# One operand of a product and a row maximum: the lattice filter of a language-model tower, rearranged between VectorE and GpSimd

## What is computed

```python
scores = q @ k.T / sqrt(64)                       # 1024 x 1024
int_scores = (abs(scores) * 1618.0).astype(int32)
penalty = where(int_scores % 3 == 0, 1 / PHI, 1)  # mod 9 in {0, 3, 6}
attn = softmax(scores * penalty)
attn = attn * (sin(C1 * attn) * exp(-attn * attn / PHI) + cos(C2 * attn))
ctx = attn @ v
```

## Time and profile before

| | us |
|---|---|
| median of 3 runs | 5857.68 |
| lowest, highest | 5852.5, 5871.76 |
| the profiled execution | 5868.64 |
| its span | 5866.9 |

### The profile page before, as it was taken

The page is one execution under the profiler, slowest core; times in us unless marked ns, Lnnn a source line. Parts: engine busy times, 40 slices in busy tenths (PEclk is TensorE's granted clock), DMA queues, the critical chain, the costliest instruction groups (busy, mean ns, idle before and its releaser), DMA issues. The chain is left out here.

```text
span 5866.9 us, 98280 instructions
## 1 busy us (share of the span) xinstructions
PE 4792.8 (82%) x27646; PEld 2698.8 (46%) x27689; DVE 4141.1 (71%) x7553; ACT 3988.8 (68%) x5466; POOL 3773.1 (64%) x3599
## 2 busy tenths in 40 slices
PE   2688888888888888888888888888888869997899
PEld 1344444444444444444444444444444436554566
DVE  2577777777777777777777777777777656665664
ACT  1577777777777777777777777777777734444332
POOL 4577777777777777777777777777777634443233
PEclk9799999999999999999999999999999879999999
DMA  0000000000000000000000000000000000000000
GB/s 5 23 9 8 8 8 8 8 9 8 10 8 8 8 8 8 8 8 8 9 8 10 8 8 8 8 8 8 8 9 8 4 9 1 2 2 15 3 6 7
DMA packets 34184, 45.24 MB, mean 8 GB/s; under 512 B 24521, under 2 KB 24585, under 8 KB 34058
## 3 DMA queue, kind: packets, MB, share of 16 engines
q1 hardware_dynamic: 32010, 43.49, 2.8%
q0 software_dynamic: 2048, 0.14, 0.1%
HBM read 39.40 MB, written 4.19 MB: 7 GB/s over the span
## 5 line engine op out<-in xcount | busy, mean ns | idle before, releaser
L588 PE MATMUL banks<-ident,att 128*128 128x128 f32 x8192 | 1148.2, 287 | 410.0 <-DVE ag L520 252.1
L588 PEld LDWEIGHTS banks<-ident,att 128*128 128x128 f32 x8192 | 944.6, 147 | 1004.1 <-DVE ag L520 616.9
L630 PE MATMUL banks<-kT,qT 128*128 128x512 f32 x2048 | 1144.8, 658 | 278.9 <-DVE mx L549 269.6
L390 POOL TENSOR_TENSOR sinb<-sinb,ag 128x1024 f32<-128x1024 f32 x512 | 1281.5, 2506 | 85.4 <-ACT sinb L461 70.4
L540 DVE SCALAR_TENSOR_TENSOR mag<-near,mag 128x512 f32<-128x512 int32 x1024 | 857.7, 842 | 483.6 <-POOL near L406 474.2
L400 POOL TENSOR_SCALAR mag<-mag 128x512 f32<-128x512 f32 x1024 | 689.5, 678 | 573.1 <-DVE mag L540 539.0
L647 PE MATMUL outp<-sinb,vo 128*64 128x512 f32 x2048 | 1046.3, 636 | 0.0
L647 PE MATMUL outp<-work,vo 128*64 128x512 f32 x2048 | 1046.3, 636 | 0.0
L406 POOL TENSOR_SCALAR near<-mag 128x512 int32<-128x512 f32 x1024 | 794.0, 775 | 363.9 <-ACT mag L479 300.3
L479 ACT ACTIVATE mag<-banks 128x512 f32<-128x512 f32 x1024 | 599.2, 592 | 283.1 <-PE banks L630 283.0
L497 DVE TENSOR_TENSOR work<-banks,work 128x1024 f32<-128x1024 f32 x512 | 625.1, 1221 | 192.8 <-ACT work L455 189.8
(11 more groups left out here) (198 smaller groups left out, 6357.7 us busy)
## 6 DMA issues: line engine op xcount, KB each, us to landing
x<-xT_dram SPq DMA_DIRECT2D x128, 256.0 KB, 3.5
xT_dram<-xT SPq DMA_DIRECT2D x8, 256.0 KB, 2.9
out<-hres SPq DMA_DIRECT2D x8, 256.0 KB, 2.6
base<-in_L_tok_turns,idx POOLq DMA_INDIRECT x64, 2.3
wqk<-in_L_attn_Wq SPq DMA_DIRECT2D x64, 16.0 KB
wqk<-in_L_attn_Wk SPq DMA_DIRECT2D x64, 16.0 KB
wqk<-in_L_attn_bq SPq DMA_DIRECT2D x64, 0.2 KB
wqk<-in_L_attn_bk SPq DMA_DIRECT2D x64, 0.2 KB
```

The costliest lines, as they stand in the source:

```text
L390: nc.gpsimd.tensor_tensor(sinb[:, k % RING], sinb[:, k % RING], ag[:, k], ALU.mult).then_inc(tmul, 1)
L588: mm = nc.tensor.matmul(turn_pair(k)[:, c, i * P:(i + 1) * P], att[:, p, 4 * half + i, kt * P:(kt + 1) * P], ident[:], is_transpose=True, ...
L630: nc.tensor.matmul(score_bank(n), qT[:, p, (n // 2) * P:(n // 2 + 1) * P], kT[:, p, (n % 2) * 512:(n % 2 + 1) * 512], start=True, stop=Tru ...
```

## The change

Three things on two engines:
- The PHI operation on POOL is gone. The comparison's 1.0 or 0.0 goes straight into a scalar_tensor_tensor on DVE, (mag + PHI) x score, which writes att and keeps no maximum.
- The maximum and the bias become one operation per block on 1024 columns of att: it multiplies by -EXPSCALE in place, and its reduction, a minimum, goes into nb. The exponential takes scale -1.0 for EXPSCALE. The tile mx is gone.
- All eight blocks are normalised on POOL; the two on DVE, their semaphore and their case are gone.

FILT moves from step +4 to +3, BIAS from +6 to +4.

```diff
-        ABS, RND, KEEP, FACT, FILT, BIAS = 1, 1, 2, 3, 4, 6
+        ABS, RND, KEEP, FILT, BIAS = 1, 1, 2, 3, 4
...
-                        if a - NORM in EXP and EXP.index(a - NORM) not in DVE_ROWS:
+                        if a - NORM in EXP:
                             j = EXP.index(a - NORM)
                             held(pool, recip, TB * g + j + 1)
                             nc.gpsimd.tensor_scalar(att[:, p, j], att[:, p, j], rs[:, j:j + 1], TURN,
                                                     ALU.mult, ALU.mult).then_inc(weights, 1)
-                        if a - FACT in SCORE:
-                            n = SCORE.index(a - FACT)
-                            held(pool, kept, NTILE * g + n + 1)
-                            nc.gpsimd.tensor_scalar(mag[:, n % 4], mag[:, n % 4], 1.0, PHI,
-                                                    ALU.mult, ALU.add).then_inc(factor, 1)
...
                             nc.scalar.activation(att[:, p, j], att[:, p, j], ACT.Exp,
-                                                 bias=nb[:, p, j:j + 1], scale=EXPSCALE,
+                                                 bias=nb[:, p, j:j + 1], scale=-1.0,
                                                  accum_out=ssum[:, j:j + 1]).then_inc(expd, 1)
...
-                        if a - NORM in EXP and EXP.index(a - NORM) in DVE_ROWS:
-                            j = EXP.index(a - NORM)
-                            wait(dve, recip, TB * g + j + 1)
-                            nc.vector.tensor_scalar(att[:, p, j], att[:, p, j], rs[:, j:j + 1], TURN,
-                                                    ALU.mult, ALU.mult).then_inc(weights2, 1)
...
-                            wait(dve, factor, NTILE * g + n + 1)
-                            wait(dve, filtered, NTILE * g + n)
+                            wait(dve, kept, NTILE * g + n + 1)
                             wait(dve, xpose, NX * (g - 1))
-                            dve.nop(nofuse=True)
-                            nc.vector.tensor_tensor_reduce(
-                                att[:, p, u, cols], mag[:, n % 4], score_bank(n), 1.0,
-                                mx[:, p, n - 1:n] if n % 2 else -3.0e38, ALU.mult, ALU.max,
-                                mx[:, p, n:n + 1]).then_inc(filtered, 1)
+                            nc.vector.scalar_tensor_tensor(att[:, p, u, cols], mag[:, n % 4], PHI, score_bank(n),
+                                                           ALU.add, ALU.mult).then_inc(filtered, 1)
...
                             wait(dve, filtered, NTILE * g + n + 1)
-                            nc.vector.tensor_scalar(nb[:, p, u:u + 1], mx[:, p, n:n + 1], -EXPSCALE, None,
-                                                    ALU.mult).then_inc(bias, 1)
+                            nc.vector.tensor_scalar(att[:, p, u], att[:, p, u], -EXPSCALE, 3.0e38, ALU.mult, ALU.min,
+                                                    accum_out=nb[:, p, u:u + 1]).then_inc(bias, 1)
...
-                wait(pe, weights, (TB - 2) * g + (TB // 2 - 1) * (half + 1))
-                wait(pe, weights2, 2 * g + half + 1)
+                wait(pe, weights, TB * g + TB // 2 * (half + 1))
```

More of the change, by code:

```diff
@@ L262, in lattice @@
         sinb = sb("sinb", [P, RING, S])
-        mx = sb("mx", [P, 2, 2 * TB])
         nb = sb("nb", [P, 2, TB])
@@ L294, in lattice @@
         NORM, TURNS = 1, 3
-        DVE_ROWS = (TB // 2 - 1, TB - 1)
         block = ctx.enter_context(nc.Block())
@@ L521, in iteration @@
                                                     ALU.mult).then_inc(agd, 1)
-                        if a - NORM in EXP and EXP.index(a - NORM) in DVE_ROWS:
-                            j = EXP.index(a - NORM)
-                            wait(dve, recip, TB * g + j + 1)
-                            nc.vector.tensor_scalar(att[:, p, j], att[:, p, j], rs[:, j:j + 1], TURN,
-                                                    ALU.mult, ALU.mult).then_inc(weights2, 1)
                         if a - TURNS in EXP:
                             j = EXP.index(a - TURNS)
-                            if j in DVE_ROWS:
-                                wait(dve, weights2, 2 * g + j // 4 + 1)
-                            else:
-                                wait(dve, weights, (TB - 2) * g + j + 1 - j // 4)
+                            wait(dve, weights, TB * g + j + 1)
                             wait(dve, nned, TB * g)
```

8 lines of the change are left out of this document (4 added, 4 removed).

## The result

The changed kernel takes 5899.74 us (median of 6 runs, 5896.79 to 5901.71) against 5860.70 us for the kernel before, run beside it: ratio 1.0073, 95% interval 1.0061 to 1.0084. It is slower by 39 us, where I had forecast 30 us less. The profiled execution took 5900.63 us, its span 5898.9.

A forecast was written before the change was run, and what follows sets the result against it. A chain across in-order queues, with POOL leading the middle piece, was taken to set the period. Terms 0.3 - 1.62 + 1.06 - 0.24 = -0.5 us per head, times 63 = -31 us, gave 5830 us, range 5710 to 5970.

The forecast's parts named there:

- step 1: From MUL 0, the head's first sine-stretch multiplication, to the end of the eighth sine product: +0.3 us, bounds 0 and +1.6.
- step 4: From AG 0 (first L520) to the next head's MUL 0, 22.79 us: -0.24 us, DVE and ACT level, bounds -1.0 and +1.0.
- step 2: From the eighth sine product's end to the last comparison before AG 0, 13.37 us: -1.62 us, bounds -3.8 and -0.5.
- Step 3: From that comparison to AG 0, the first L520: +1.06 us, from 1.35 to 2.41, bounds +0.5 and +1.4.
- middle piece: The 19.48 us of a head up to AG 0: POOL leads, busy 17.1 us, and the change should help there.
- VectorE's account: DVE's work per head: products 9.6 and BIAS 9.1 added, 10.8 and 2.2 removed, net +5.7 us.
- rival C: BIAS runs at two columns a step: -1.05 us per head, about 5790 us; chance 0.06.
- GpSimd's account: POOL's work per head: sixteen L400 go, two normalisations L395 come, -8.0 us.
- rival B: Slower, the delay at MUL 2 in the sine stretch not absorbed: +0.8 us per head, 5908 us; chance 0.35.
- A: Rival: the relief of POOL comes through, -2.2 us per head, about 5720 us; chance 0.22.
- the absorbed case: The forecast itself: MUL 2's delay in the sine stretch mostly absorbed, 5830 us, own range 5780 to 5875; chance 0.37.
- My sign for DVE as the bound: The stretch from AG 0 to the next MUL 0 growing beyond 23.5 us would show that DVE is the bound.

The follow-up runs named there:

- run 5: Kernel before without L400: the addition of PHI left out, the product reading the comparison's 1.0 or 0.0; 5692.9 us, ratio 0.9727.
- run 7: Changed kernel with the BIAS of blocks 5 and 7 two steps later, behind MUL 2 and MUL 7; 5842.2 us, ratio 0.9979.
- run 6: Kernel before without L400's addition of PHI and with all eight blocks normalised on POOL; 5784.2 us, ratio 0.9885.
- run 4: Changed kernel with each BIAS over 512 of 1024 columns and an exponential scale of -1e-6; 5808.6 us, ratio 0.9926.
- run 11: Changed kernel with the eight BIAS at steps chosen one by one where DVE waits, none behind AG 0; 5833.9 us, ratio 0.9966.

## Why the prediction was wrong

Two steps failed. Over both heads of the pair step 1 lost 0.92 us, where I had 0.3, and step 4 lost 0.55, where I had -0.24; steps 2 and 3 came out within 0.03. That is 0.62 + 0.79 of the 1.4 us per head between the forecast of -0.5 and the measured +0.9. With either step as forecast the change would still not have been faster (+0.3 or +0.1 us per head).

- **What bounds the kernel.** Right in its middle piece. Without L400 step 2 falls by 3.0 us and the kernel by 163 (run 5): POOL did lead there, and DVE no longer waits for L400.
- **VectorE's account.** The sum is right, +5.5 us per head against +5.7. BIAS is at 1.13 in the queue (1.14 from start to start, 2530.70 to 2531.84), the product at 0.60 (x2 in 1.19). Two parts that I left out cancel: the comparisons, more of which lie beside POOL's operations, went from 853 to 919 ns on average in the pair, and the roundings, of half the number, from 824 to 716.
- **The page.** All 512 BIAS operations lie between 1.201 and 1.221 us; 319 of them lie beside a running POOL instruction, as that at 2530.70 beside the L388 of 2530.34. The Gaussian product over as many columns takes 1.212. So it runs at one column a step and nobody blocks it. The Trainium skill (SBUF — State Buffer, "Who interferes with whom"), which excepts the accumulator form from the shared pair, agrees with the trace; the Trainium skill's VectorE: DVE Perf Modes ("The perf-mode tier table"), read without that exception, does not, and rival C is out.
- **GpSimd's account.** -9.5 us per head for -8.0: roundings and sine products also got shorter, from 775 to 687 and from 2506 to 2427 ns on average.
- **Step 1 failed.** I took the 1.6 us by which MUL 2 would be late, let PE's later waits swallow 0.4 and a shorter second rounding 0.5, and wrote +0.3, so that another 0.4 has no reason in my text. MUL 2 and the PE work behind it were late by 1.64 us, as I had worked out. The rounding did become shorter (1.12 to 0.67 us), but it now waited 0.53 us for ACT, so this gave nothing. Nothing was swallowed in even heads (+1.65, my upper bound 1.6), nearly all in odd ones (+0.19). What hid it in the odd ones is no wait of PE for L549 but the clock: the odd head before had already lost 1.46 us at MUL 5 to a low stretch, 18.98 against 17.52, and the delayed MUL 2 puts MUL 5 at 19.16 in every head, with or without one (table in run 7). I had read the steps in one head, the even one, whose clock is 1.00, and my text offered what one head shows and the other may hide as a reason against rival B; it is true of the odd head alone. Run 7 shows the cause of 1.1 of the 1.65 us: the same operations, two of them moved, -1.13 us at MUL 2 and at MUL 5, and -1.14 in step 1 of even heads.
- **Step 2 right:** -1.64 for -1.62, though by compensation: -2.99 for L400 (I had -3.77), +1.06 for a normalisation (run 6 against run 5; I had 1.70), and +0.28 for what DVE has queued (the change against run 6; I had 0.45).
- **Step 3 right:** +1.07 for +1.06.
- **Step 4 mis-sized:** +0.55 for -0.24, inside its bounds. I counted DVE to 22.5 us with ACT level with it. The terms that I listed, from the 20.61 us busy, add up to 22.9 and not to 22.5, and DVE is busy 22.91 of 23.34 us. The three BIAS in it are the cause in the odd heads: with half of their columns step 4 is back at 22.61 us (run 4), with none of them in it at 22.58 (run 11), for 22.66 before and 23.22 in the change. In the even heads the comparison blocked by block 7's normalisation adds to DVE's work (0.75 us), and the low stretch that every even head had there before is gone in 7 of 19; those take 23.07 us, the others 23.36.
- **The rivals.** B was right in its mechanism for the even heads, and near in its price: 5908 for 5900. The nearness is in part luck. B had +1.6 us in step 1 of every head and left step 4 at -0.24; measured are +0.92 on average and +0.55, and the two errors cancel. Its condition, more than 0.5 us beyond my terms in steps 1 and 4, was met with 1.35 + 0.79 us in even heads and 0.79 in odd ones, less the -0.11 of the odd step 1. A failed: steps 3 and 4 are now DVE's (2.42 of 2.42 and 22.91 of 23.34 us), and POOL leads only in step 2. My forecast gave the absorbed case 0.37 and B 0.35 on the same row, PE busy 25.0 of 27.16 us in the stretch behind MUL 2. PE's share alone could not decide it: over step 1 it was 28.5 of 31.9 us in the even head and 30.2 of 33.1 in the odd one, which hid the delay.
- **What would show it.** BIAS, the product and the PE instruction 1.64 us later came as said. POOL's idle time per pair grew by 21 us, not 15 (36.6 to 57.4). The comparison that closes step 2 was to be 1.3 us earlier after MUL 0 and AG 0 0.3 earlier: in odd heads they are (1.45 and 0.39), in even ones the comparison stays and AG 0 is 1.1 later. My sign for DVE as the bound, a step 4 beyond 23.5 us, did not come (23.34 and 23.21), though DVE is the bound there; the limit was too far out.

## What to carry to other kernels

When one operation of 1.1 us replaces several short ones in an in-order queue, look at what stands right behind its place before you count its time: here two steps of delay for two of eight placements gave some 55 us back, more than the 39 that the kernel had lost, and by the rows one of the two placements did it. Before you write that a delay is absorbed, find the row that shows what absorbs it, in both heads of an alternating rhythm: here it was a stretch at the lower clock, which only one of the two had, and which an edit can move. The shorter head has the most to lose. Compare heads with as many low stretches as each other; only so could the effect of a place be told from that of the clock. Work moved to an engine costs what its stretch allows, not what it takes: the same two normalisations cost 211 us on a loaded POOL, 91 with L400 gone and 30 with DVE loaded too.
